# Half of the ordering of gates moves from the routing block into the first routed blocks; gathers go from the smallest slot up; four down projections are loaded earlier

## The reference, cut to what matters

```python
tidx, tw = _route(xf, router_w, correction_bias)      # 8 of 64 experts per token, 2.5 * normalised gates
combine = zeros((T, 64)).at[arange(T)[:, None], tidx].add(tw)
acc = acc + c[:, None] * (relu2(xf @ wu) @ wd)         # for each expert, c = its column of combine
shared = relu2(xf @ shared_up_w) @ shared_down_w       # for all tokens
x = x + tanh(g_ffn[0]) * (routed + shared)
```

## Time and profile before

| | us |
|---|---|
| median of 3 runs | 2625.3 |
| lowest and highest run | 2624.1, 2625.47 |
| the profiled execution's own time | 2619.68 |
| its span in the profile | 2617.9 |
| TensorE busy in the span | 2320.2 |
| VectorE busy | 2104.3 |
| ScalarE busy | 1518.0 |
| GpSimd busy | 1800.0 |

### The profile page before, as it was taken

The page is one execution under the profiler, slowest core; times in us unless marked ns, Lnnn a source line. Parts: engine busy times, 40 slices in busy tenths (PEclk is TensorE's granted clock), DMA queues, the critical chain, the costliest instruction groups (busy, mean ns, idle before and its releaser), DMA issues. The chain is left out here.

```text
span 2617.9 us, 41338 instructions
## 1 busy us (share of the span) xinstructions
PE 2320.2 (89%) x11459; PEld 1289.8 (49%) x11459; DVE 2104.3 (80%) x3593; ACT 1518.0 (58%) x2536; POOL 1800.0 (69%) x1569
## 2 busy tenths in 40 slices
PE   2999899999989999998999899999997958999990
PEld 1444444444544444444444444444444647988770
DVE  5687688988897897889889878988896775688884
ACT  3666666666665666666666656666662423666660
POOL 3787576679858885887698688858875630077776
PEclk9999999999999999999999999999997989999995
DMA  8434333221111111111211111111115408799994
GB/s 301 170 105 167 114 125 101 77 79 43 59 46 59 55 59 46 59 44 53 79 43 57 48 57 56 60 46 57 45 55 172 150 1 305 243 321 325 328 319 141
DMA packets 163129, 305.71 MB, mean 117 GB/s; under 512 B 19842, under 2 KB 99138, under 8 KB 160194
## 3 DMA queue, kind: packets, MB, share of 16 engines
q1 hardware_dynamic: 134786, 235.40, 26.5%
q0 software_dynamic: 24576, 67.14, 7.7%
q10 hardware_dynamic: 3520, 0.27, 0.1%
HBM read 172.99 MB, written 129.76 MB: 116 GB/s over the span
## 5 line engine op out<-in xcount | busy, mean ns | idle before, releaser
L1147 POOL TENSOR_SCALAR e<-e 128x1024 f32<-128x1024 f32 x520 | 682.2, 1312 | 364.5 <-ACT e L1043 311.2
L1043 ACT ACTIVATE e<-scores 128x1024 f32<-128x1024 f32 x520 | 533.2, 1025 | 443.8 <-PE scores L908 437.1
L1336 DVE TENSOR_TENSOR e_sum<-e_sum,e 128x1024 f32<-128x1024 f32 x391 | 612.7, 1567 | 107.7 <-POOL e L1147 103.1
L965 PE MATMUL ps_o<-e,v 128*64 128x512 f32 x2088 | 570.3, 625 | 6.8 <-POOL e L1147 6.8
L908 PE MATMUL scores<-q_t,k_t 64*128 64x512 f32 x3120 | 512.6, 434 | 14.4 <-ACT affine L1020 12.7
L908 PEld LDWEIGHTS scores<-q_t,k_t 64*128 64x128 f32 x3120 | 257.9, 188 | 378.5 <-issue 313.4
L1870 POOL DMA_INDIRECT more<-results_in_blocks,index x256 | 246.4, 962 | 210.6 <-DMA results_in_blocks<-more 129.4
L1055 ACT ACTIVATE k_sw<-ps_k 32x512 f32<-32x512 f32 x512 | 301.2, 588 | 83.5 <-PE ps_k L939 78.7
L1132 POOL DMA_INDIRECT rows_in_blocks<-room,a_r_index_now x192 | 265.5, 1383 | 49.0 <-issue 42.1
L939 PE MATMUL ps_k<-ctx_t,wqk 128*128 128x512 f32 x768 | 222.9, 427 | 12.5 <-DVE q_t L1308 12.2
L924 PE MATMUL ps_v<-wv,ctx_t 128*128 128x512 f32 x768 | 212.1, 411 | 0.0
(11 more groups left out here) (294 smaller groups left out, 3612.3 us busy)
## 6 DMA issues: line engine op xcount, KB each, us to landing
rows_in_blocks<-room SPq DMA_DIRECT2D x16, 2560.0 KB, 10.1
x_nat<-rows_in_blocks SPq DMA_DIRECT2D x160, 256.0 KB, 5.2
results_in_blocks<-more SPq DMA_DIRECT2D x80, 512.0 KB
wqk<-wqk_pairs SPq DMA_DIRECT2D x65, 512.0 KB, 3.5
wv<-wv_quads SPq DMA_DIRECT2D x17, 1024.0 KB, 4.9
wo<-in_L_xattn_Wo SPq DMA_DIRECT2D x66, 128.0 KB, 3.4
x_nat<-in_ctx SPq DMA_DIRECT2D x8, 1024.0 KB, 7.7
down_all<-in_L_ffn_down_w SPq DMA_DIRECT2D x16, 512.0 KB, 8.2
```

The costliest lines, as they stand in the source:

```text
L965: mm = pe.matmul(ps_o[hh * DH:(hh + 1) * DH, :], v[:, tile, buf, hh * DH:(hh + 1) * DH], e[:, tile % 4, hh * N:(hh + 1) * N], start=(tile ...
L1043: act.activation(e[:, c % 4], scores[:, c % 2], ACT.Exp, scale=SCALE).then_inc(s_exp, 1)
L1147: pool.tensor_scalar(e[:, c % 4], e[:, c % 4], EXP_HI, EXP_LO, ALU.min, ALU.max).then_inc(s_clip, 1)
L1336: dve.tensor_tensor(total, e[:, 0] if c == 2 else total, e[:, tile % 4], ALU.add).then_inc(s_sum, 1)
```

## The change

Tiles 0 to 15 are now ordered in `experts` and tiles 16 to 31 in `finish_routing`, all by VectorE alone. `more` is laid out in quarters (slots and gates of tiles 0 to 15, slots and gates of tiles 16 to 31), so that the tables of the first sixteen lie where the gathers will land; GpSimd waits for the 48 operations of their ordering before its first gather. The operations go one behind the square of each of blocks 0 to 47. A batch's gathers go through the sorted slots from the last (smallest) to the first, with a wait for the stored results that lets the first four go four blocks earlier. The down projections of experts 0 to 3 are loaded a second time, in `finish_routing`, into the place of `router.rows`; blocks 0 to 3 use these.

```diff
+LATER = T_T // 2
@@ Router
     def gathered(self):
-        self.slot_all = self.kept.more_part(0, T_T, E_R)
-        self.gate_all = self.kept.more_part(T_T * E_R, T_T, E_R)
+        n = LATER * E_R
+        self.slot_all = [self.kept.more_part(2 * half * n, LATER, E_R) for half in range(2)]
+        self.gate_all = [self.kept.more_part((2 * half + 1) * n, LATER, E_R) for half in range(2)]
+
+    @staticmethod
+    def of_tile(whole, t):
+        return whole[t // LATER][:, t % LATER]
@@ finish_routing, SP
             for whole, dram in ((router.slot_all, slots_dram), (router.gate_all, gates_dram)):
-                sp.dma_start(whole[:, 0:last * GT].rearrange("p (g t) e -> p g (t e)", t=GT),
-                             dram.rearrange("g p n -> p g n")).then_inc(all_loaded, 16)
+                for half, groups in enumerate((range(0, LATER // GT), range(LATER // GT, last))):
+                    sp.dma_start(whole[half][:, 0:len(groups) * GT].rearrange("p (g t) e -> p g (t e)", t=GT),
+                                 dram[groups[0]:groups[-1] + 1].rearrange("g p n -> p g n")).then_inc(all_loaded, 16)
...
             for k in range(GT):
                 sp.wait_ge(router.scattered[k], 16 * TOP_K * N_G)
+            sp.dma_start(router.rows, ins["down_w"][0:CHUNK].rearrange("e p n -> p e n")).then_inc(kept.first_loaded, 16)
             for i in range(0, XR, XC):
@@ finish_routing, GpSimd
-            for n, t in enumerate(by_pool):
-                c = pool_cells[:, n % 2]
-                pool.wait_ge(cells_equal, n + 1)
-                pool.tensor_tensor(c, c, router.gate_all[:, t].unsqueeze(1).broadcast_to([P, TOP_K, E_R]), ALU.mult
-                                   ).then_inc(cells_ready, 1)
@@ finish_routing, VectorE
-            dve.wait_ge(all_loaded, 32)
-            scale_gates(slice(0, last * GT))
-            dve.wait_ge(gates_ready, 1)
+            dve.wait_ge(all_loaded, 64)
+            scale_gates(slice(0, LATER))
+            scale_gates(slice(LATER, last * GT))
+            dve.wait_ge(gates_ready, 2)
...
-            order(range(0, 3))
+            order(range(LATER, LATER + 3))
...
-            order(range(3, 6))
+            order(range(LATER + 3, LATER + 6))
             shared(4)
             normalise(7)
-            order(range(6, 9))
+            order(range(LATER + 6, LATER + 9))
             shared(5)
-            order(range(9, 13))
+            order(range(LATER + 9, LATER + 13))
             shared(6)
-            order_with_pool(by_pool[0:5])
+            order(range(LATER + 13, T_T))
             shared(7)
-            order_with_pool(by_pool[5:16])
-            order(range(13, 16))
@@ experts
+        kept.taken_up = 2 * N_G * E_R
+        first_down = kept.part(CHUNK, D)
         now_up = kept.part(4, D)
+        cells = sb("e_cells", [P, TOP_K, E_R])[:]
...
+        def choice(q):
+
+            return q // TOP_K, TOP_K - 1 - q % TOP_K
+
+        def blocks_of(b, k):
+
+            return -(-(E_R + (b + 1) * BODY - k) // YC) * YC
@@ experts, TensorE, back(i)
-                    if i % CHUNK == 0:
+                    if i == 0:
+                        pe.wait_ge(kept.first_loaded, 16)
+                    elif i % CHUNK == 0:
                         pe.wait_ge(down_loaded[i // CHUNK], 16)
-                    w = down[:, i]
+                    w = down[:, i] if i >= CHUNK else first_down[:, i]
...
+                    if i == E_R:
+                        pe.wait_ge(down_loaded[0], 16)
@@ experts, VectorE
             def combine(q, b):
-                t, k = b * GT + q // TOP_K, q % TOP_K
+                t, k = b * GT + choice(q)[0], choice(q)[1]
                 dve.wait_ge(y_in[k], t * 16 + 16)
-                if k:
+                if q % TOP_K:
                     dve.wait_ge(added, b * BODY + q)
...
+            def order(n):
+                t, part = n // 3, n % 3
+                each = [P, TOP_K, E_R]
+                if n:
+                    dve.wait_ge(ordered, n)
+                if part == 0:
+                    st = dve.tensor_tensor(cells, router.of_tile(router.slot_all, t).unsqueeze(1).broadcast_to(each),
+                                           kept.key[:, t].unsqueeze(2).broadcast_to(each), ALU.is_equal)
+                elif part == 1:
+                    st = dve.tensor_tensor(cells, cells, router.of_tile(router.gate_all, t).unsqueeze(1).broadcast_to(each), ALU.mult)
+                else:
+                    st = dve.tensor_reduce(kept.gate8[:, t], cells, mybir.AxisListType.X, ALU.add)
+                st.then_inc(ordered, 1)
...
                 dve.tensor_tensor(act_g[:, i % 4], act_r[:, i % 2], act_r[:, i % 2], ALU.mult).then_inc(s_g, 1)
+                if i < 3 * LATER:
+                    order(i)
                 late = i - E_R - BODY - LAG
@@ experts, GpSimd
             def gather(b):
-                for k in range(YR // YC):
-                    pool.wait_ge(y_stored[k], (b * BODY + E_R + BODY) // YR * 16)
                 for q in range(BODY):
-                    t, k = q // TOP_K, q % TOP_K
+                    t, k = choice(q)
+                    n = blocks_of(b, k) // YC
+                    if q in (0, YC):
+                        for group in (n - 2, n - 1):
+                            pool.wait_ge(y_stored[group % (YR // YC)], (group // (YR // YC) + 1) * 16)
                     if b * BODY + q >= TOP_K:
                         pool.wait_ge(added, b * BODY + q - TOP_K + 1)
                     at = kept.index[:, b * GT + t, k:k + 1]
-                    pool.indirect_dma_start(land[:, k], None, y_dram[0:(E_R + (b + 1) * BODY) * P, :], bass.IndirectOffsetOnAxis(ap=at, axis=0)
+                    pool.indirect_dma_start(land[:, k], None, y_dram[0:blocks_of(b, k) * P, :], bass.IndirectOffsetOnAxis(ap=at, axis=0)
                                             ).then_inc(y_in[k], 16)
 
+            pool.wait_ge(ordered, 3 * LATER)
             for b in range(B):
                 gather(b)
```

More of the change, by code:

```diff
@@ L156, in __init__ @@
         self.x_loaded = [ctx.enter_context(nc.semaphore(f"xs_loaded_{k}")) for k in range(XR // XC)]
+        self.first_loaded = ctx.enter_context(nc.semaphore("first_down_loaded"))
         self.taken_up = 0
@@ L548, in keep_last @@
         for whole, now in ((self.slot_all, self.slot), (self.gate_all, self.gate)):
-            st = act.activation(whole[:, (N_G - 1) * GT:N_G * GT], now[:], ACT.Copy)
+            st = act.activation(whole[1][:, LATER - GT:LATER], now[:], ACT.Copy)
         st.then_inc(kept, 1)
@@ L1358, in finish_routing @@
         last = N_G - 1
-        by_pool = range(T_T // 2, T_T)
         RING = 3
@@ L1387, in finish_routing @@
         table_made, table_out, table_in = sem("table_made"), sem("table_out"), sem("table_in")
-        gates_ready, cells_equal, cells_ready = sem("gates_ready"), sem("cells_equal"), sem("cells_ready")
+        gates_ready = sem("gates_ready")
         all_loaded, last_kept = sem("all_loaded"), sem("last_kept")
@@ L1556, in scale_gates @@
                 n = tiles.stop - tiles.start
-                gates = router.gate_all[:, tiles]
+                gates = router.gate_all[tiles.start // LATER][:, tiles.start % LATER:tiles.start % LATER + n]
                 done(dve.tensor_reduce(total[:, tiles], gates, mybir.AxisListType.X, ALU.add))
@@ L1567, in order @@
                     c = cells[:, t % 2]
-                    done(dve.tensor_tensor(c, router.slot_all[:, t].unsqueeze(1).broadcast_to([P, TOP_K, E_R]),
+                    done(dve.tensor_tensor(c, router.of_tile(router.slot_all, t).unsqueeze(1).broadcast_to([P, TOP_K, E_R]),
                                            kept.key[:, t].unsqueeze(2).broadcast_to([P, TOP_K, E_R]), ALU.is_equal))
-                    done(dve.tensor_tensor(c, c, router.gate_all[:, t].unsqueeze(1).broadcast_to([P, TOP_K, E_R]), ALU.mult))
+                    done(dve.tensor_tensor(c, c, router.of_tile(router.gate_all, t).unsqueeze(1).broadcast_to([P, TOP_K, E_R]), ALU.mult))
                     done(dve.tensor_reduce(kept.gate8[:, t], c, mybir.AxisListType.X, ALU.add))
[L1573 to L1588, removed]
             def table():
@@ L1652, in _, with experts @@
             scale_gates(slice(last * GT, N_G * GT))
-            dve.wait_ge(gates_ready, 2)
+            dve.wait_ge(gates_ready, 3)
             normalise(6)
-            order(range(3, 6))
+            order(range(LATER + 3, LATER + 6))
             shared(4)
             normalise(7)
-            order(range(6, 9))
+            order(range(LATER + 6, LATER + 9))
             shared(5)
-            order(range(9, 13))
+            order(range(LATER + 9, LATER + 13))
             shared(6)
-            order_with_pool(by_pool[0:5])
+            order(range(LATER + 13, T_T))
             shared(7)
-            order_with_pool(by_pool[5:16])
-            order(range(13, 16))
-def experts(nc, pers, ins, out, kept, up, xs_dram, y_dram):
```

(9 more changed lines are left out.)

1 line of the change is left out of this document (removed).

## The result

The changed kernel takes 2597.3 us (median of 4 runs, 2595.9 to 2599.7) against 2624.7 for the kernel before on the same chip (4 runs, 2622.7 to 2625.5): ratio 0.9898, 95% interval 0.9881 to 0.9915, so 27.4 us less (22 to 31 by the interval).

A forecast was written before the change was run, and what follows sets the result against it. An ordering hole with TensorE idle, then a chain from first combine through 247 gathers, was taken to bound the kernel. -26.2 + 4.2 = -22.0 us gave 2597.7 profiled, plus 5.6 for the median: 2603.3, range 2598 to 2614.

The forecast's parts named there:

- the last one: From profiled execution to median: the kernel before's 5.6 us difference, added to 2597.7, gives 2603.3.
- (a): End of finish_routing: without ordering behind the last shared addition, the block ends at 2136.43 instead of 2162.68, -26.2 us.
- the 3.02 of the earlier trace: Idle time at the boundary from attention to finish_routing, the upper bound for the boundary into experts; +2.5 in the range.
- (b): Blocks 0 to 47 of experts: one ordering operation each, 1.31 us per block; first 28 unchanged, next 20 cost +4.2 us.
- (c): Early load of the first four down projections in finish_routing: covered, no bytes saved, 0.
- (d): Gathers from the smallest slot up: first gather 4.4 us earlier, ninth waits 7.4 for the first combine; 0, at best -0.7.
- A: Rival: VectorE runs operations without overlap in the 48 blocks, 1.60 us each; net -10.6, 2615 us; chance 0.10.
- B: Rival: in experts' first 28 blocks, waits for rows and VectorE's work add up; net -14.4, 2611 us; chance 0.12.
- C: Rival: the full DMA phase in experts shortens to VectorE's own pace; -24.5, 2601 us, inside the main case (0.69).
- E: Rival: something else holds the boundary between finish_routing and experts, so nothing changes; 2625 us, chance 0.04.
- D: Rival: TensorE falls to its lower clock during the 48 blocks; net +11.3, 2637 us, chance 0.05.
- The end moves with the first combine: Chain in experts: first combine, 247 gathers at 1.27 us each, landing, out; the end moves as the first combine does.

The follow-up runs named there:

- move_only: Changed kernel with the gathers' old order and wait and without the early down-projection load: 2742.5 us, ratio 0.9900; again in a later session 2599.6 us, ratio 0.9900.
- order_late_again: Changed kernel with the 48 ordering operations behind blocks 32 to 79 instead of 0 to 47: 2606.2 us, ratio 0.9923 to the kernel before.
- order_twice_again: Changed kernel with the 48 ordering operations done a second time behind blocks 48 to 95, sums unread: 2605.6 us, ratio 0.9933 to the kernel before.
- LAG 8: Changed kernel with LAG 8 instead of 16, so combines start at block 104: 2593.9 us (ratio 0.9880) and 2591.9 us (0.9890) in two normal sessions.

## Why the prediction was right or wrong

**The step that failed is the last one: "The median of the three runs is 2625.3, 5.6 above that execution; the difference applies to it as well."** For the profiled execution the text gives 2597.7 and the profile measured 2595.89; those 1.8 us are the earlier last addition. But the changed kernel's median lies only 1.4 above its profiled execution, and 0.3, 0.5 and 0.2 above it in the three last sessions, not 5.6. The miss of 6.0 us (2603.3 against 2597.3) is these two: 1.8, and 4.2 for the 5.6 that were 1.4. Both profiled executions of the kernel before (2619.68, 2618.78) lie some 6 us under its median; the second is the lowest of its 8 runs, of which the next is 2622.2. A time carried from one traced execution to a median has an error of some 5 us here, and the low end of the range, with only 2 us outside the terms of the changed stretch, had no room for it. Over four measurements outside the second session the medians' differences are 27.4, 22.3, 24.5 and 25.6, 25 in the mean; from the last shared addition to the end the traces show 22.9. Whether the 2 us between them are chance, or something before the change that profiles of the kernel before do not catch, stays open.

**(a) The hole** was right: 26.75 us from the last shared addition to the first DMA of experts became 0.29. The three tiles ahead of the last group hid, as that addition still follows 2.64 us of waiting for TensorE, and the boundary costs no more than before (0.29 us, where 0.5 was taken); the 3.02 of the earlier trace rows was not the nearest row.

**(b) The ordering inside experts** was right in mechanism and within a microsecond in each stretch: 0.60 us per operation as forecast, 1.29 per block against 1.31, 28 blocks in 40.7 against 40.9, 20 in 25.8 against 26.2. One thing was left out: when the ordering ends, tiles of TensorE stand ready and VectorE makes up some 1.1 us of the lag (five blocks in 4.4 us). From the first DMA of experts the first combine is 2.9 us later than before (136.7 against 133.9), where +4.2 was forecast. Another 1.7 were lost between the first combine and the end (322.6 against 320.9; 320.2 to 321.5 in the later profiles, 319.8 in the other of the kernel before), which reads as spread. So the sum of -22.0 met -21.9 partly by luck: 1.3 less than forecast to the first combine and 1.7 more behind it. One reading of the prediction was off without anything hanging on it: 9.04 us for 7 gathers are 1.29 each and not 1.25, since some gathers lasted 1.12 and 1.05; single steps between them take 1.25.

**(c) and (d)** were right at 0 together: move_only. The ninth gather's wait was forecast at 7.4 and is 7.20.

**The rivals.** A and B would have shown 48 blocks in 75 to 80 us; there were 66.5. C fell, as the first 28 blocks kept their 40.7 us, and E with the hole. D fell: the granted clock is 1.00 with TensorE busy 23.11 of 28 us. The section of the Trainium skill that the prediction named for D ("TensorE: Matmul & The Clock Gate", section "HAM oscillation — how this bites in real kernels") tells of matmul work that is shorter than the waits between it. Here the work is longer, some 1.10 us in each 1.31 by the prediction's own terms, so that section gave no reason to expect a slower end, and the trace shows none of its oscillation. "The end moves with the first combine" held in order_late_again and order_twice_again within 0.4 us, and ceases to hold once combines come early enough (LAG 8: first combine 8.8 to 8.9 earlier, end 7.2 to 7.6) or once the blocks set the pace, in the second session.

## What to carry to other kernels

Work that an engine does alone at a barrier can go into a stretch whose pace something else sets, and its price is the time from its start to the next instruction's start, less what that stretch leaves idle; here 33 us of VectorE (48 operations of 0.69) put the first combine 2.9 us later. Before an early start is counted as a gain, ask what the ring behind it waits for: the earlier first gather only lengthened the ninth's wait, and became worth something when the combines were moved too. Forecast a difference of stretches, and give a median that comes from one traced execution the spread of everything that lies before the stretch.

## What had not been expected

The program has a condition in which all versions of it take 5% longer, on at least two chips, one of which also gave the normal times in another session: TensorE stands 2.2 us at "issue" before single matmuls, and steps between gathers grow from 1.27 to 1.63 us while each gather still keeps GpSimd busy for 0.95. And outside that condition, the same program reaches the same instruction in the last shared group with 7.4 us of spread between executions, more than most edits of this study moved.
